# GpSimd waits, one square root, the mask's spread products and one table load rearranged around the first expert layer

## The reference

```
x = x + _L0_xattn_ref(_layernorm(x), ctx_768, ...)      # one head of width 128
x = x + _L0_ffn_ref(_layernorm(x), ...)                 # 8 experts, the best one alone
x = x + _L1_xattn_ref(_layernorm(x), ctx_768, ...)      # 8 heads of width 64
x = x + _L1_ffn_ref(_layernorm(x), ...)                 # 32 experts, 4 chosen, and a shared one
```

```
logits = xt @ Wg.T
top1 = jnp.argmax(logits, axis=-1)
def body(y, p):
    h = jax.nn.gelu((xhat * s_e + b_e) @ w1 + bb1, approximate=False)
    out = h @ w2 + bb2
    mask = (top1 == eid)[:, None].astype(out.dtype)
    return (y + mask * out, None)
```

## Time and profile before

| | us |
|---|---|
| median of 3 runs (lowest to highest) | 1462.4 (1462.14 to 1464.22) |
| the profiled execution's own time | 1464.52 |
| its span, first to last instruction | 1462.7 |
| TensorE busy | 1391.6 (95%) |
| VectorE busy | 1095.5 (75%) |
| GpSimd busy | 941.2 (64%) |
| ScalarE busy | 793.9 (54%) |
| mean granted TensorE clock | 0.954 |

### The profile page before, as it was taken

How to read it: one execution, slowest core, us unless ns; L and a number is a source line. 1 busy time by engine, 2 the same in 40 slices (tenths; PEclk the granted TensorE clock), 3 DMA queues, 4 the chain that set the end, 5 groups by cost and what they waited for, 6 DMA issues and landing times.

```text
span 1462.7 us, 19933 instructions
## 1 busy us (share of the span) xinstructions
PE 1391.6 (95%) x6191; PEld 793.8 (54%) x6191; DVE 1095.5 (75%) x1484; ACT 793.9 (54%) x1576; POOL 941.2 (64%) x542
## 2 busy tenths in 40 slices
PE   5999998887999999999999999999999999998898
PEld 3877775533455555555554555455555555554565
DVE  8976666388888788778868878887887886666555
ACT  3458886321556556556655655555555555553332
POOL 5001113231889888978988897898898899886110
PEclk8999999655999999999999999999999999998799
DMA  6630000310000200100020020002002000000011
GB/s 173 206 126 18 18 17 7 71 22 2 0 1 1 49 1 1 33 17 1 1 49 1 1 46 4 1 1 49 1 0 47 1 1 1 1 1 13 18 38 40
DMA packets 77372, 39.45 MB, mean 27 GB/s; under 512 B 62047, under 2 KB 70000, under 8 KB 77002
## 3 DMA queue, kind: packets, MB, share of 16 engines
q1 hardware_dynamic: 77290, 38.36, 10.5%
HBM read 24.66 MB, written 13.68 MB: 26 GB/s over the span
## 4 chain that ended last, share of the span: by engine, by line
PE 86%; DVE 8%; DMA 3%; ACT 2%; issue 1%; POOL 0%; SPq 0%; ACTq 0%; DVEq 0%; POOLq 0%
PE ps L1384 24%; PE ps L1371 14%; PE ps L1372 12%; PE ps L1337 9%; DVE chunk_max L943 3%; DMA v_scratch<-v_stage 3%; PE ps L1324 3%; PE ps L1528 2%; PE ps L1199 2%; PE ps L1197 2%; PE ps L1208 2%; PE ps L1198 2%; PE ps L1209 2%; PE ps L1210 2%; PE ps L1316 1%
## 5 line engine op out<-in xcount | busy, mean ns | idle before, releaser
L524 POOL TENSOR_TENSOR psums<-psums,probs 126x1024 f32<-126x1024 f32 (+1 forms) x392 | 821.2, 2095 | 122.6 <-ACT probs L705 75.7
L705 ACT ACTIVATE probs<-ps 126x512 f32<-126x512 f32 (+1 forms) x816 | 416.2, 619 | 273.2 <-PE ps L1372 272.3
L943 DVE TENSOR_REDUCE chunk_max<-ps 128x2 f32<-128x1008 f32 (+1 forms) x416 | 472.7, 1181 | 77.1 <-PE ps L1337 75.7
L1384 PE MATMUL ps<-probs,v_mem 126*64 126x512 f32 (+1 forms) x1632 | 389.7, 598 | 0.0
L1371 PE MATMUL ps<-q_heads,ring 128*126 128x512 f32 (+1 forms) x816 | 342.9, 420 | 1.1
L1372 PE MATMUL ps<-q_low,ring 128*126 128x512 f32 (+1 forms) x816 | 322.5, 395 | 0.0
L994 DVE TENSOR_TENSOR xn<-xn,probs 126x512 f32<-126x512 f32 x126 | 231.1, 1834 | 29.9 <-ACT probs L705 25.6
L671 ACT CAST ring<-ps 64x252 fp32r<-64x252 f32 (+1 forms) x356 | 128.1, 360 | 136.3 <-PE ps L1324 133.2
L1384 PEld LDWEIGHTS ps<-probs,v_mem 126*64 126x64 f32 (+1 forms) x1632 | 111.5, 136 | 165.5 <-issue 120.9
L1371 PEld LDWEIGHTS ps<-q_heads,ring 128*126 128x126 f32 (+1 forms) x816 | 152.0, 186 | 88.6 <-issue 44.5
L1337 PE MATMUL ps<-ring,q_heads 64*128 64x504 f32 (+1 forms) x416 | 171.9, 482 | 18.1 <-DVE chunk_max L943 9.7
(11 more groups left out here) (200 smaller groups left out, 1412.8 us busy)
## 6 DMA issues: line engine op xcount, KB each, us to landing
v_scratch<-v_stage SPq DMA_DIRECT2D x51, 252.0 KB
v_mem<-v_scratch SPq DMA_DIRECT2D x8, 1606.5 KB
ctx_mem<-in_ctx_t SPq DMA_DIRECT2D x3, 803.2 KB, 8.9
vslot<-in_ctx_rows SPq DMA_DIRECT2D x51, 47.2 KB
pair_w<-in_f_pairs SPq DMA_DIRECT2D x17, 128.0 KB, 2.1
pair_w<-in_f_pairs SPq DMA_DIRECT2D x17, 65.0 KB, 1.8
x_tok<-in_x SPq DMA_DIRECT2D x1, 512.0 KB, 4.1
wo<-in_c_wo SPq DMA_DIRECT2D x1, 512.0 KB
```

The lines of the kernel that those rows point to most:

```text
L524: pool.tensor_tensor(sums[0:r, 0:width], sums[0:r, 0:width], probs[0:r, n % PROBS, 0:width], ALU.add).then_inc(c_sum, 1)
L705: act.activation(probs[0:r, n % PROBS, cols(half)], ps[0:r, score_bank(t, half), :], ACT.Exp, scale=float(HD) ** -0.5).then_inc(c_exped, 1)
L943: dve.tensor_reduce(chunk_max[:, h % 2, i:i + 2, c], ps[:, banks[0]:banks[1] + 1, 0:group_tiles(c) * KT], AX, ALU.max).then_inc(c_reduced, 1)
L1384: ins = pe.matmul(ps[half * HD:(half + 1) * HD, B_ACC, :], v_tiles[0:r, h % 2, t, :], probs[0:r, n % PROBS, cols(half)], start=(t == 0), s ...
```

## The change

- `EARLY` becomes (3, 3, 5). Group 5 is no longer made ahead of normalization 2's turn but in the stage of maxima, which now makes groups 5 to 14. ScalarE takes normalization 2's square root behind group 3 and ahead of group 4, and GpSimd waits for normalization 2 and adds the bias ahead of group 5.
- Ahead of its subtraction for group 1 GpSimd waits for all of normalization 1.
- The mask and the spreading matrix get copies of type float32r, and the four products of line 1290 take these. The bias products read the same memory as float32. ScalarE rounds `spread0` behind the first attention; TensorE's wait ahead of the bias sums of line 1259 counts that copy too.
- Behind `q_rows(1)` ScalarE computes one exponential of a column of zeros that nobody reads.

```diff
-EARLY = (3, 3, 6)
+EARLY = (3, 3, 5)
@@ memory
-        mask_t = v_mem[0:E0, 5 * TOK:6 * TOK]
+            spread0_r = sb_a("spread0_r", [E0, G0, P], F32R)
+            mask_r = sb_a("mask_r", [E0, TOK], F32R)
+        mask_t = mask_r[:, :].bitcast(F32)
@@ gpsimd, the early groups
                 pool.wait_ge(c_kfull, g + 1)
+                if g == 1:
+                    pool.wait_ge(ln_out, 2 * TT)
                 pool.tensor_tensor(ring[HD:P, g, 0:n, 1, :], k_full[:, g % 2, 0:n, :], f32(ring[HD:P, g, 0:n, 0, :]),
                                    ALU.subtract).then_inc(c_klo_first, 1)
@@ scalar
+            act.wait_ge(in_f0, 16 * 9)
+            act.copy(spread0_r[:, :, :], spread0[:, :, :]).then_inc(f_w, 1)
             for j in range(CH):
                 act.wait_ge(a_vout[j], 16 * CHUNKS)
             k_first(0)
...
-                        ins = act.copy(mask_t[:, cols(part)], ps[0:E0, B_MASK[part], :])
+                        ins = act.copy(mask_r[:, cols(part)], ps[0:E0, B_MASK[part], :])
...
             q_rows(1)
+            act.activation(first_std[:, :], zero_col[:, :], ACT.Exp)
@@ tensor
-            pe.wait_ge(f_w, 2)
+            pe.wait_ge(f_w, 3)
...
-                pe.matmul(ps[:, B_SPREAD[n], :], spread0[:, g, :], mask_t[:, cols(half)], start=True, stop=True).then_inc(f_pe, 1)
+                pe.matmul(ps[:, B_SPREAD[n], :], spread0_r[:, g, :], mask_r[:, cols(half)], start=True, stop=True).then_inc(f_pe, 1)
```

## The result

The changed kernel takes 1453.5 us (median of 5 runs, 1452.76 to 1456.45) against 1462.63 before (1462.14 to 1464.22): ratio 0.9941, 95% interval 0.9925 to 0.9956. Two more times it was run beside the kernel before: 1455.19 and 1455.24 against 1462.94, ratios 0.9956 (0.9943 to 0.9969) and 0.9944 (0.9931 to 0.9957). By the ratios it is faster by 6 to 9 us. The profiled execution took 1452.76 us, its span is 1451.0.

A forecast was written before the change was run, and what follows sets the result against it. TensorE was 86% of the chain; in the stretch that changes, whichever engine was last bound it. Terms: 1.52 + 2.5 + 0.6 + 2.04 - 0.25 + 0 = 6.4 us, from median 1462.4 to 1456.0 us; range 1452.9 to 1459.5.

The forecast's parts named there:

- Normalization 1: VectorE's eight scaled tiles before the logits, with GpSimd waiting behind them: 2.14 us instead of 3.66, 1.52 us gained.
- Rounding the spreading matrix: New ScalarE copy of 8 rows by 256, in a 3.62 us idle gap of ScalarE: costs nothing.
- Spread products: Mask's spread in the first expert layer: four one-pass products instead of eight float32 instructions, 2.5 us gained.
- The clock in that block: TensorE's clock over the 48 instructions of bias rows and down projection: 0.6 us gained, bounds -3.7 to +4.0 us.
- the second's: Rival: the clock's rise falls later in the work, the block costs 3 us more; 1459.6 us, chance 0.12.
- The first rival: Clock never falls, bias rows and down projection run at full speed: 9.5 us gained, 1452.9 us; chance 0.12.
- Square root: Normalization 2, ScalarE's root ahead of group 4: starts at 281.94 instead of 283.98, 2.04 us gained.
- Bias and group 5: GpSimd's bias addition of 2.34 us after normalization 2, now with group 5 behind it: no effect.
- A tenth group: Stage of maxima, ten groups instead of nine: 0.25 us lost, bounds 0 and 2.0.
- Exponentials' table: ScalarE's 1.28 us table load behind the first scores moves into idle time: 0 gained, up to 1.28.
- The slower rival: TensorE stays at half clock into the head loop: 1465.2 us with 20 us of extra half clock; chance 0.03.

## Why the prediction was right, and where it was off

The time lies in the range, 2.5 us under the 1456.0 forecast; in the two repeats it was 0.8 under. Most of the hit is mechanism: three terms came as summed. Part is luck: the block's clock gave four times what was put down for it. In the profiles the stretch from the first scaled tile of normalization 1 to the first maxima product is 8.8 us shorter, where 6.6 were forecast, and not the whole difference lies there: 1.1 us lie behind it, besides the 1.8 ahead of it.

- *Normalization 1*, 1.52 us: 1.52 measured, and 1.53 alone. That constants cost something beside the subtraction is shown too: of the 1.52 us the subtraction took 1.0 and two writes of constants 0.5. So the prediction's remark that 1.52 us were gone where one subtraction overlapped put too much on it: its share stays below its own length of 1.22 us.
- *Rounding the spreading matrix*, 0: the copy took 0.40 us at 241.29, and ScalarE still sat idle for 3.33 us behind it.
- *Spread products*, 2.5 us: 3.63 - 1.12 = 2.51. VectorE's four products took 2.48 us in a row and did stay ahead.
- *The clock in that block*, 0.6 us taken from a range of -3.7 to +4.0: this is the term that was mis-sized. The 48 instructions gained 8.8 - 5.6 = 3.2 us, the mask's turn, more of it at half clock, lost 0.7; net 2.5. All of the 48 are at full clock now, and the half clock fell on the mask's turn ahead of them, so both rivals' mechanisms show, the second's with 0.7 us. My reason for taking only a quarter was wrong. The profiled execution of before did not have more of the half clock in this block than others: the block took 12.5 us in each of five. What made that execution slow lay in the first attention (250.84 us to normalization 1, the longest of fourteen). The first rival, that the clock never falls behind fewer shallow products, was the better forecast for this block; the reason for it stood in the text and it got 0.12. That the time still lies in the range is because the range had been drawn out to that rival.
- *Square root*, 2.04 us: the distance from aggregation to square root fell from 2.08 to 0.03. The eight tiles kept their stretched length, 3.15 us, as said. By the Trainium skill (ScalarE: Activation LUTs, What ACT_TABLE_LOAD costs) a drain should have left half of the gain; the load ended at 273.23, the aggregation at 273.55 and the square root began at 273.58, so no drain of 1.4 us is in the trace.
- *Bias and group 5*, nothing: right, but it was more than nothing in the other direction. Without moving group 5 the root alone gives 1.1 us. The prediction held its removal to be off the path; it is what keeps GpSimd's constants and TensorE's projection out of normalization 2.
- *A tenth group*, 0.25 us lost: 0.3 to 0.4 between profiles of like clock. The stage as a whole was 0.55 us shorter instead, and VectorE's waits for TensorE in it sum to 2.8 us where 3.5 + 0.25 were forecast; the clock at its start fits that. The last early group's copy ended 13 reductions before the stage did, not ten, with the same result.
- *Exponentials' table*, 0: 0. The first exponential starts 351.49 - 347.04 = 4.45 us after the row maxima instead of 5.72, and the loop keeps its length.

The slower rival had no run near it: the head loop took 984.8 to 985.7 us in thirteen of fourteen profiles, and 986.9 in the last. (By its own terms the prediction's chance of a faster kernel was 0.66 + 0.07 + 0.12 + 0.06 = 0.91, not 0.90.)

## What to carry to other kernels

Where the path runs through a chain of small steps, cost each from a disturbed and an undisturbed copy of the same step in the same trace; here that gave three terms (1.52, 2.5 and 2.04 us) to a tenth of a microsecond. Price the clock as a mechanism with its own place: look at what kind of products stood before each fall, and how far ahead of them the clock had risen, in several profiles, not at how slow one execution was. When a step is moved ahead of a group of work, ask what the group behind it now lies over.

## What was not expected of the hardware

Behind four float32 products 8 rows deep (eight instructions, 3.6 us), and the first of the shallow bias rows, TensorE's clock fell from 2.4 to 1.2 GHz although TensorE was busy without a pause (6.86 of 6.90 us), in five of five profiles; behind the same products padded to 128 rows with zeros it did not, in one profile. Writing constants on GpSimd slowed VectorE's scaling of SBUF tiles too, by 0.5 us over two writes of 0.55 and 0.62 us, half of the 1.0 us that a subtraction of 1.22 us cost.
